# One 256 KB load for two tiles and both choices, weights and bias on ScalarE's queue, the second choice weighed on ScalarE

## What is computed

```
x = x + 0.5 * moe(layernorm(x))          # 8 experts, 2 chosen per token, 128 -> 512 -> 128, gelu
x = x + decay_attention(layernorm(x))    # one head, scores * 0.99^distance, causal, no softmax
x = x + 0.5 * moe(layernorm(x))
x = x + 0.5 * fp4_ffn(layernorm(x))      # 128 -> 352 -> 128, operands rounded to 4-bit steps
x = x + bias_attention(layernorm(x))     # 16 heads of 64, relative position bias, softmax
x = x + 0.5 * fp4_ffn(layernorm(x))
```

## Time and profile before

| What | us |
|---|---|
| Three executions | 3148.33, 3150.88, 3151.51 |
| Their median | 3150.88 |
| The profiled execution's own time | 3141.97 |
| Its span in the profile | 3139.9 |
| A0, from its first load's issue to VectorE's last instruction | 549.0 to 699.7 |
| C1, from its first load's issue to VectorE's last instruction | 1233.5 to 1342.8 |

### The profile page before, as it was taken

The page is one execution under the profiler, slowest core; times in us unless marked ns, Lnnn a source line. Parts: engine busy times, 40 slices in busy tenths (PEclk is TensorE's granted clock), DMA queues, the critical chain, the costliest instruction groups (busy, mean ns, idle before and its releaser), DMA issues. The chain is left out here.

```text
span 3139.9 us, 67679 instructions
## 1 busy us (share of the span) xinstructions
PE 2377.1 (76%) x17707; PEld 1936.7 (62%) x17708; DVE 2312.1 (74%) x8343; ACT 1810.8 (58%) x4746; POOL 1397.5 (45%) x1366
## 2 busy tenths in 40 slices
PE   2328884673348882058859999999999999997787
PEld 2328784453348772036647877878787787875565
DVE  4427786885338774768858888888888888887786
ACT  2214442333224441135529999999999999997554
POOL 3755665005746654025514444444444444443454
PEclk9999997885579996578869999999999999998888
DMA  4133332302133333300000000000000000000000
GB/s 152 52 94 104 108 106 74 102 17 109 52 104 108 110 108 106 96 7 0 0 29 7 5 3 3 3 3 3 3 3 3 3 3 3 3 4 1 10 20 24
DMA packets 144714, 137.32 MB, mean 44 GB/s; under 512 B 20084, under 2 KB 130484, under 8 KB 143844
## 3 DMA queue, kind: packets, MB, share of 16 engines
q1 hardware_dynamic: 127204, 100.31, 10.5%
q0 software_dynamic: 17408, 35.82, 3.5%
HBM read 59.31 MB, written 44.24 MB: 33 GB/s over the span
## 5 line engine op out<-in xcount | busy, mean ns | idle before, releaser
L2039 POOL TENSOR_TENSOR p_prob<-p_prob,p_inverse 128x512 f32<-128x512 f32 x512 | 533.0, 1041 | 760.9 <-DVE p_inverse L1863 760.9
L1956 ACT ACTIVATE p_prob<-p_neg,p_neg_max 128x256 f32<-128x256 f32 x1024 | 508.7, 503 | 1.6 <-DVE p_neg_max L1857 1.6
L1867 DVE SCALAR_TENSOR_TENSOR p_probT<-p_t_ps,p_probT 128x512 f16<-128x512 f32 x512 | 353.3, 690 | 153.9 <-ACT p_probT L1962 153.0
L868 ACT ACTIVATE p_e_hT<-p_e_h_ps,p_b 128x256 f32<-128x256 f32 x576 | 226.3, 475 | 305.9 <-PE p_e_h_ps L818 291.2
L982 POOL DMA_INDIRECT results_by_token<-p_e_result,p_e_slot x288 | 283.6, 985 | 247.8 <-DVE p_e_result L928 172.6
L1857 DVE CUSTOM_DVE_ANT_0 p_neg<-p_s_ps,top_bias 128x256 f32<-128x256 f32 x1024 | 388.4, 417 | 0.7 <-ACT p_prob L1956 0.6
L692 POOL DMA_INDIRECT rows_by_expert<-p_r_z,p_r_target x256 | 250.2, 977 | 308.4 <-DVE p_r_z L552 185.5
L1962 ACT ACTIVATE p_probT<-p_t_ps 128x512 f16<-128x512 f32 x512 | 305.4, 597 | 71.2 <-PE p_t_ps L2107 69.8
L827 PE MATMUL p_e_o_ps<-p_w,p_e_hT 128*128 x2304 | 300.1, 286 | 46.6 <-issue 30.6
L827 PEld LDWEIGHTS p_e_o_ps<-p_w,p_e_hT 128*128 128x128 f32 x2304 | 281.7, 200 | 59.7 <-issue 59.4
L2107 PE MATMUL p_t_ps<-top_ident,p_prob 128*128 128x128 f32 x2048 | 307.5, 273 | 2.4 <-POOL p_prob L2039 2.4
(11 more groups left out here) (265 smaller groups left out, 6214.2 us busy)
## 6 DMA issues: line engine op xcount, KB each, us to landing
p_e_affine<-p_affine SPq DMA_DIRECT2D x144, 192.0 KB, 2.2
p_e_z<-rows_by_expert SPq DMA_DIRECT2D x144, 129.0 KB, 2.2
p_got<-results_by_token SPq DMA_DIRECT2D x256, 64.0 KB, 1.8
results_by_token<-p_e_result,p_e_slot POOLq DMA_INDIRECT x288
p_r_w<-in_w SPq DMA_DIRECT2D x2, 2048.0 KB, 7.9
p_w<-in_w SPq DMA_DIRECT2D x2, 2048.0 KB, 11.8
rows_by_expert<-p_r_z,p_r_target POOLq DMA_INDIRECT x256, 2.3
p_reversed<-bias_by_distance SPq DMA_DIRECT2D x2, 2048.0 KB, 12.5
```

The lines of the kernel that those rows point to most:

```text
L1867: v.scalar_tensor_tensor(probT[k % 2][:, 1, :, :], t_ps[k % 2][:], PROB_SCALE, probT[k % 2][:, 0, :, :], ALU.mult, ALU.subtract).then_inc( ...
L1956: ins = act.activation(prob[k % PROBS][:, t, :], neg[k % 2][:, t, :], ACT.Exp, bias=neg_max[k % 2][:, t:t + 1], scale=-1.0, accum_out=tota ...
L2039: pool.tensor_tensor(prob[k % PROBS][:], prob[k % PROBS][:], inverse[k % PROBS][:].unsqueeze(2).to_broadcast([P, SEQ_TILES, SEQ]), ALU.mult)\
```

## The change

The rows of `results_by_token` are numbered anew: choice k of token (tile t, row p) lies in row (2t + k) * 128 + p, so that a tile's two choices lie behind each other. One load now brings two tiles with both choices (256 KB, still as pieces of 512 bytes), with two semaphores (`landed[h]`) in place of four: 2 loads for a group in place of 8. A half's load waits until the same half of the group before has landed. On ScalarE, `weigh_second` multiplies choice 1 by its gate, in place, with 4 activations for a group. VectorE adds choice 0 as before (4 instructions), waits for `weighted`, and adds the 4 weighed tiles with one tensor_tensor of 128x512. In A0 ScalarE weighs groups 0 to 2 ahead of everything, group 3 ahead of `projections(0)`, and group i+4 in iteration i ahead of `normalise(i + 3)`; the loop is peeled at its end by 4 groups in place of 3. In C1 the bias's and weights' loads are issued from ScalarE's queue, with `position.keep` now ahead of `position.skew` in the same program; ScalarE then weighs groups 0 to 7, reverses the bias, keeps the weights, and weighs groups 8 to 15. SyncE's queue in C1 has the combine's loads alone.

```diff
--- before.py
+++ after.py
@@ -288,18 +288,25 @@
                     act.wait_ge(v_done, i + 2)
                 if there(i, 2):
                     turned(i + 2)
+                if combine and there(i, 4):
+                    combine.weigh_second(act, i + 4)
                 if there(i, 3):
                     normalise(i + 3)
 
+            if combine:
+                for i in range(3):
+                    combine.weigh_second(act, i)
             normalise(0)
             turned(0)
             normalise(1)
+            if combine:
+                combine.weigh_second(act, 3)
             act.wait_ge(loaded, 64)
             projections(0)
             act.wait_ge(v_done, 1)
             turned(1)
             normalise(2)
-            loop_and_peel(act, 0, 3, body)
+            loop_and_peel(act, 0, 4, body)
 
         @block.tensor
         def _(pe):
@@ -1001,45 +1008,65 @@
 class Combine:
 
 
+    HALVES = 2
+    HALF = GT // HALVES
+
     def __init__(self, x_res, routes, dram_results):
         self.x_res, self.gate = x_res, routes["gate"]
-        self.results = dram_results[0:TOP_K * TOKENS, :].rearrange("(k t p) d -> p t k d", p=P, k=TOP_K)
+        self.results = dram_results[0:TOP_K * TOKENS, :].rearrange("(n p) d -> p n d", p=P)
 
     def allocate(self, m, groups):
         self.groups = groups
-        self.got = m.sb("got", [P, groups * GT, TOP_K, D])
-        self.landed = [m.sem(f"landed{r}") for r in range(GT)]
-        self.added_one, self.added = m.sem("added_one"), m.sem("added")
+        self.got = m.sb("got", [P, groups * GT * TOP_K, D])
+        self.landed = [m.sem(f"landed{h}") for h in range(self.HALVES)]
+        self.weighted, self.added_one, self.added = m.sem("weighted"), m.sem("added_one"), m.sem("added")
         self.carried = m.sem("carried")
 
     def load(self, sp, i, first):
-        for r in range(GT):
+        for h in range(self.HALVES):
             if not (isinstance(i, int) and i == 0):
-                sp.wait_ge(self.landed[r], i * (16 * TOP_K))
+                sp.wait_ge(self.landed[h], i * 16)
                 sp.sem_inc(self.carried, 1)
-            if r == 0 and first > 0:
+            if h == 0 and first > 0:
                 sp.wait_ge(self.added, i - (first - 1))
                 sp.sem_inc(self.carried, 1)
-            at = bass.ds((i - first) * GT + r, 1)
-            for k in range(TOP_K):
-                sp.dma_start(self.got[:, at, k, :], self.results[:, bass.ds(i * GT + r, 1), k, :]).then_inc(self.landed[r], 16)
+            rows = self.HALF * TOP_K
+            sp.dma_start(self.got[:, bass.ds((i - first) * (GT * TOP_K) + h * rows, rows), :],
+                         self.results[:, bass.ds(i * (GT * TOP_K) + h * rows, rows), :]).then_inc(self.landed[h], 16)
+
+    def of_tile(self, i, first, r, k):
+        return self.got[:, bass.ds((i - first) * (GT * TOP_K) + (r * TOP_K + k), 1), :].rearrange("p t d -> p (t d)")
 
     def load_all(self, sp):
         self.load(sp, 0, 0)
         loop_groups(sp, 1, self.groups, lambda i: self.load(sp, i, 0))
         loop_groups(sp, self.groups, GROUPS, lambda i: self.load(sp, i, self.groups))
 
+    def weigh_second(self, act, i, first=0):
+        for r in range(GT):
+            if r % self.HALF == 0:
+                act.wait_ge(self.landed[r // self.HALF], i * 16 + 16)
+            t = bass.ds(i * GT + r, 1)
+            got = self.of_tile(i, first, r, 1)
+            ins = act.activation(got, got, ACT.Copy, scale=self.gate[:, 1, t])
+        ins.then_inc(self.weighted, 1)
+
     def add(self, v, i, first=0):
-        for k, done in enumerate((self.added_one, self.added)):
-            for r in range(GT):
-                if k == 0:
-                    v.wait_ge(self.landed[r], i * (16 * TOP_K) + 16 * TOP_K)
-                t = bass.ds(i * GT + r, 1)
-                x = self.x_res[:, t, :].rearrange("p t d -> p (t d)")
-                got = self.got[:, bass.ds((i - first) * GT + r, 1), k, :].rearrange("p t d -> p (t d)")
-                ins = v.scalar_tensor_tensor(x, got, self.gate[:, k, t], x, ALU.mult, ALU.add)
-            ins.then_inc(done, 1)
-            v.wait_ge(done, i + 1)
+        for r in range(GT):
+            if r % self.HALF == 0:
+                v.wait_ge(self.landed[r // self.HALF], i * 16 + 16)
+            t = bass.ds(i * GT + r, 1)
+            x = self.x_res[:, t, :].rearrange("p t d -> p (t d)")
+            got = self.of_tile(i, first, r, 0)
+            ins = v.scalar_tensor_tensor(x, got, self.gate[:, 0, t], x, ALU.mult, ALU.add)
+        ins.then_inc(self.added_one, 1)
+        v.wait_ge(self.weighted, i + 1)
+        v.sem_inc(self.carried, 1)
+        v.wait_ge(self.added_one, i + 1)
+        xg = self.x_res[:, bass.ds(i * GT, GT), :]
+        second = self.got[:, bass.ds((i - first) * (GT * TOP_K), GT * TOP_K), :].rearrange("p (t k) d -> p t k d", k=TOP_K)[:, :, 1, :]
+        v.tensor_tensor(xg, xg, second, ALU.add).then_inc(self.added, 1)
+        v.wait_ge(self.added, i + 1)
         v.sem_inc(self.carried, 1)
 
 
@@ -1664,9 +1691,6 @@
 
         @block.sync
         def _(sp):
-            position.load(sp)
-            weights.load(sp)
-            position.skew(sp)
             if combine:
                 combine.load_all(sp)
 
@@ -1677,9 +1701,21 @@
 
         @block.scalar
         def _(act):
+            position.load(act)
+            weights.load(act)
             position.keep(act)
+            position.skew(act)
+
+            def weigh_groups(first, last, base):
+                loop_groups(act, first, last, lambda i: combine.weigh_second(act, i, base))
+
+            if combine:
+                combine.weigh_second(act, 0)
+                weigh_groups(1, GROUPS // 2, 0)
             position.turn_round(act)
             weights.keep(act)
+            if combine:
+                weigh_groups(GROUPS // 2, GROUPS, GROUPS // 2)
 
         @block.vector
         def _(v):
@@ -2251,7 +2287,7 @@
     bucket_of = (np.arange(BUCKETS)[:, None] == bucket[None, :]).astype(np.float32)
 
     row = np.arange(P)[:, None, None]
-    token_slots = np.arange(TOP_K)[None, None, :] * TOKENS + np.arange(TILES)[None, :, None] * P + row
+    token_slots = (np.arange(TILES)[None, :, None] * TOP_K + np.arange(TOP_K)[None, None, :]) * P + row
     spare_slots = TOP_K * TOKENS + np.arange(SPARE_TILES)[None, :] * P + np.arange(P)[:, None]
 
     return {"bucket_of": bucket_of, "ident": np.eye(P, dtype=np.float32), "decay": decay.astype(np.float32),
```

## The result

| | before | after |
|---|---|---|
| Median of five executions, us | 3151.51 | 3136.26 |
| Range | 3148.33 to 3153.51 | 3129.49 to 3142.12 |
| The profiled execution's own time | 3141.97 | 3136.26 |
| Its span | 3139.9 | 3134.2 |

The ratio is 0.9954, with a 95% interval of 0.9938 to 0.9971: the change gains some 15 us. Predicted were 3113, between 3104 and 3130. The time lies 6 us above the range.

What follows compares the result with a forecast made beforehand. It took SyncE's load issues, and late first loads, to bound C1, and VectorE to bound A0. Gains of 30.9 and 6.75 us, 37.6 together, off 3141.97 gave 3104.3 us profiled, 3113 as a median; range 3104 to 3130.

Steps and rivals of the forecast that it cites:

- The change part by part: Sum of gains over the whole kernel: C1 30.9 us, A0 6.75 us, renumbered rows nothing; 37.6 us in all.
- The last rival: Change does not do what it says (loads split again or a dependence kept): gain of 10 to 25 us; 4%.
- signs of being wrong: Groups slower than 4 us, ScalarE's first multiplication in C1 held beyond 1250, or A0's iteration staying at 8.6 us.
- the cover of 2 us for the loads: C1's first half: bytes at 290 GB/s are in by 1266, group 7 is wanted at 1268; 2 us spare.
- the crowding rival: C1's first half: long 2 MB issue delays weighing 4.3 us; group 3 lands behind the 4 MB, 3 us; 3120 us; 20%.
- as the ring filled: C1: reason given for the second 2 MB load's issue taking 2.0 us against 0.38; 1 us more assumed.
- The larger load: Results' loads in A0 and C1: a 256 KB load lands in 2.5 us, bounded by 1.8 and 6.6 us.
- the rival of the other sign: C1 and A0: two loads in flight are too few; from no change (3144 us) to slower (3235 us); 7%.
- What speaks against the move to ScalarE's queue: C1: whether results' loads can overtake the 4 MB issued from another queue; with nothing overtaking, group 3 would wait.
- A0: 2.1 for 6.75: A0: VectorE's shorter second addition saves 0.45 us for each of 15 groups, 6.75 us.
- The waits of the last three iterations stay: End of A0's loop: the waits in its last three iterations were taken as unchanged.
- The carry from profile to median: Whole kernel: plain-run median lies 8.9 us (0.28%) above the profiled execution; same difference added, 3104.3 to 3113 us.

Runs made afterwards that it cites:

- e7: Kernel before with only the bias's and weights' loads moved to ScalarE's queue, loads still 64 KB: C1 98.6 us against 110.8, median 3269.6 us (one run).
- e6: Changed kernel plus 23 VectorE increments ahead of A1, bias's and weights' loads back on SyncE: C1 93.3 us against 83.6, median 3273.37 us (one run).
- e3: Kernel before with 165 semaphore increments added on VectorE at the start of A1: A1 1301.2 us, median 3292.15 us, 8.8 us above the kernel before.
- e1: Changed kernel with 23 semaphore increments added on VectorE at the start of A1: A1 1291.7 us, ratio to the kernel before 0.9905.

## Why the prediction was wrong

The sum was 3104.3 us for a profiled execution; it took 3136.3. The 32 us are A1 18.3, F1 5.1, A0 4.7 and C1 3.7, the rest 0.2.

- **"The change part by part": nothing was counted outside A0 and C1.** This is the step that failed: a term for A1 was left at nothing, and it measured 18.3 us. The prediction took an untouched phase for an unchanged one. Shortening `Combine.add` moved VectorE's loop of A1 23 instructions forward, over the edge of a block, and the loop pays 1.5 us in each iteration. Without it the median would be near 3136.3 - 19.6 = 3117 us, inside the range; on one chip it was measured as 20.8 us. No rival had this form, and none could bring a loss from outside the two phases. The last rival names 10 to 25 us, but by loads split again or a dependence kept, and neither is there (64 loads of 256 KB, groups at 3.31 us). None of the prediction's signs of being wrong appeared either: all of them looked at C1 and A0.
- **C1: right in mechanism, 27.2 in place of 30.9.** The second addition of group 0 came 13.1 us after the start (12.5 predicted), groups at 3.31 us (3.38), the wait behind the quantising was 4.54 us (4.4). The quantising began 42.2 us after the start in place of 38.0: the cover of 2 us for the loads did not hold, group 4's two halves were late by 4.1 us together. The cover was a sum of bytes, but two loads in flight took 7.2 to 8.6 us to land beside the 4 MB, in place of 2.9. That is the second half of the crowding rival (3 us, predicted for group 3). ScalarE's issue of the two 2 MB loads took 3.01 us, the second 2.5 and not 7.3, so its first half did not come; that such an issue is long "as the ring filled" is shown by no run.
- **The larger load: 2.9 us for 2.5.** Harmless: two in flight were enough, and the rival of the other sign is out. Loads are no longer what sets a group's 3.31 us.
- **What speaks against the move to ScalarE's queue.** By the rule that the Trainium skill's page "DMA: Bandwidth & Descriptors" has in the section quoted there, read as nothing overtaking, group 3 would have waited for the 4 MB; no run bears that out, and that section of the Trainium skill has DMAs of all issuers interleave, which the trace agrees with. Groups 3 and 4 are added from 1252.85 and 1257.50 on, with loads issued from 1241.16 on, while the 2 MB loads, issued at 1239.8 and 1240.3, took 13.1 and 20.4 us to land (median 16.8, before 12.5): each is slowed, and neither waits for the other. On one queue, in before, the first results' load was issued at 1242.63 and used at 1256.31, behind the 4 MB. e7 and e6 give the move 12.2 and 9.7 us.
- **A0: 2.1 for 6.75.** Four things. The iteration gained 0.35, not 0.45: the statistics now wait 0.25 us for the one wide addition, where they had followed the last of four without a row for it, and the 0.18 in front is gone. The gain holds for 12 intervals, not 15: 4.2 us. And the last three residual sums now wait for TensorE 3.69, 3.08 and 1.29 us, before 2.10, 3.04 and 1.30: 1.6 us given back. "The waits of the last three iterations stay" was wrong for the first of them. The last 0.5 us went between the last of these sums and M1's first instruction.
- **The carry from profile to median.** 8.9 us were added since before's profiled execution was that much under the median. After's is its median, and F1, at a clock of 0.83 in place of 0.85, accounts for 5 of them. I read the offset as belonging to an execution and not to a kernel; two profiled executions don't show more.

## What to carry to other kernels

After an edit that adds or drops instructions, compare every phase with its former time, also those with untouched source; a wait put down to "issue" at one fixed place of each iteration, together with more packets on the instruction queue, points to where the loop stands, and a few idle instructions ahead of it can move it. An edit that frees the start of a phase should be priced with the transfers that it then meets: here e7's freed 20 us bought 12, because from its first addition on the first half then took 5.8 us longer beside the 4 MB of bias and the second 2 us, and putting the bias behind the half that needs the loads, with the kept weights last, was worth 6 us more than the changed kernel's C1 (77.4 against 83.6). Keep the last engine's remaining work in view when reordering, since the end of the phase passed to ScalarE.

## What the runs showed of the hardware that was not expected

- 23 instructions more or fewer, none of them doing work, move this kernel by 20 us (0.6%): 1037.5 against 1017.1 us for the same loop of 344 VectorE instructions. The change from slow to fast lies between 0 and 4 added instructions.
- A packet of the instruction queue carries 8,192 bytes (1.01 MB / 123 by the list of queues). A loop that refetches takes five of them per iteration, one at a time: in after 1.0, 3.5 and 5.9 us behind the jump, then two with some 126 instructions between them; in e3 the last three are 120 and 131 instructions apart. By the Trainium skill's section named above the unit is 16 KiB, the loop holds two and needs three. The trace differs: what it fetches at once is half of that, some 128 instructions. Counted so (an estimate, with the 11 from above), every loop that doesn't touches three such units and the two loops that refetch, after's and e3's, four. The Trainium skill's count puts each of these loops on the same side, so no run here tells which of the two rules holds where they part.
- The same refetching in e3 (125 packets, a stall of 2.1 us per iteration) costs next to nothing: 1017.5 us. The count of packets alone does not give the loss; it comes when the stalls of an iteration are longer than what VectorE has to spare, here some 2.1 us.
- 165 semaphore increments on VectorE took about 16 us (1731.3 to 1747.52), some 0.1 us each. The 23 of e1 cost A1 nothing, since VectorE waits 7.5 us for ScalarE there anyway.
